# A graph network on one core: the count matrix kept in f16 in DRAM, its row sums made in the convolution

## The chip, the cores and the metric

The kernel runs on one core of one Trainium2 chip. The metric is device time in microseconds. The core has five engines that run in parallel, each in its own order: TensorE (PE, with its weight loads as PEld), VectorE (DVE), ScalarE (ACT), GpSimd (POOL) and SyncE (SP), which here only issues DMAs. GpSimd issues the indirect DMAs. They meet through semaphores.

## What is computed

Four graph layers on 3125 nodes with 256 features and 53125 edges (`src`, `dst`, sorted by `dst`), each with a layer norm and a residual. First two attention convolutions, joined and put through an ELU-like function and a product; then five message-passing layers with batch norm; then the layer that the change also touches; then a gated edge network. What matters here is the third:

```python
def _L2_gnn_ref(x, edge_index, W, b):
    row, col = edge_index[0], edge_index[1]
    h = x @ W + b
    agg = segment_sum(h[col], row, num_segments=n)
    deg = segment_sum(ones, row, num_segments=n)
    return agg * where(deg > 0, 1 / max(deg, 1), 0)[:, None]
```

With a matrix C, in which C[s, d] is the number of edges from s to d, `agg` is C h and `deg` is the row sum of C. The message-passing layers use C as well, the other way round. C has 3200 x 3200 entries after padding (NP = 3200, in NT = 25 tiles of P = 128 nodes).

## The kernel before

The program is a chain of stages. Between them stands a barrier; inside them each engine runs its own list.

1. **Zero and histogram.** SyncE loads `dst` and `x`, then writes zeros over `count_dram`, an f32 matrix of KD = NP * NP entries in DRAM, from a tile `zeros` of 128 x ZF f32 elements that GpSimd sets (NZ = KD / (P * ZF) = 40 writes, loop L205). VectorE and TensorE make a histogram of `dst` meanwhile. VectorE's operations on `iota_row` wait for GpSimd's iotas, which come behind the memset of `zeros`.
2. **Plan and tables.** The edges are put in steps of 128 (S = 440 steps, in G4 = 110 groups of 4), with keys src * NP + dst, and score and attention tables are written to DRAM.
3. **First edge stage** (L670 to L900). For each group GpSimd gathers four blocks of scores (`score_g`, L772) and issues two accumulating scatters into `count_dram` (L792), an element of `number` to an address of `place` for each of 128 edges. Before each scatter it waits for `placed`, the landing of the one before. VectorE finds equal keys and so `number_all` and `place_all`; ScalarE copies them to `number` and `place`.
4. **Second edge stage** (L905 to L1140). The same with four gathers of attention rows (`row_g`, L980) and two scatters (L1000) a group; TensorE and VectorE sum the messages.
5. **Finish of the attention** (L1152 to L1273), five rounds of five tiles. In the first half of a round VectorE makes `val` and `neg` of five tiles (L1213 to L1221), with an exponential on ScalarE in each (L1245) and a transpose on TensorE (L1265). In the second half ScalarE copies `valT` (L1249), TensorE multiplies it with `wu` (L1271) and VectorE adds the result to `x_sb` (L1226), tile by tile: the copy of the next tile needs the next transpose, which TensorE has behind the product. In the same stage the count matrix is converted: SyncE loads a half tile of 128 x 1600 f32 counts (`cnt`, L1180), ScalarE turns it to f16 and sums its rows (`half` and `deg_half`, L1240), SyncE stores it to `by_src` (L1186), 50 times. ScalarE has one such conversion behind each of its exponentials and copies.
6. **Message passing** reads `by_src` as 128 x 25 x 400 f16 pieces.
7. **Convolution** (L1676 to L1770). For each tile SyncE loads 128 rows of `by_src` (`rows`, L1690), TensorE turns them in five pieces (L1703) and multiplies them with the node features (L1708), VectorE takes the pieces from PSUM (`take`, L1752), ScalarE takes the low half of the product (`low_sums`, L1737), and VectorE's `finish(t)` adds the halves (L1756) and adds the result, scaled with a column of `inv_deg`, to `x_sb` (L1758). `inv_deg` is made of `degsrc` for all tiles in the stage ahead.
8. The gated edge network, which also reads `degsrc`.

Of the kernel before, what the change touches and what calls it, by code (L numbers as in the profile page):

```python
# [6 lines left out]
F32 = mybir.dt.float32  # L7
# [9 lines left out]
P = 128  # L17
N = 3125
NT = -(-N // P)
NP = NT * P  # L20
# [16 lines left out]
ZF = 2000  # L37
# [13 lines left out]
HALF = NP // 2  # L51
# [53 lines left out]
def program(nc, a, out):  # L105
# [9 lines left out]
    with top:  # L115
# [47 lines left out]
        zeros = sb("zeros", [P, ZF], F32, early)  # L163
# [14 lines left out]
        count_dram = dram("count_dram", [KD + P, 1], F32)  # L178
        by_src = dram("by_src", [NP, NP], F16)
# [518 lines left out]
        with ExitStack() as ctx:  # L698
# [13 lines left out]
            number = [sb(f"number{q}", [P, 2], F32, ctx) for q in range(2)]  # L712
# [194 lines left out]
        with ExitStack() as ctx:  # L907
            with ExitStack() as inner:
                idx = [sb(f"b_idx{q}", [P, 4], I32, inner) for q in range(2)]
                number = [sb(f"b_number{q}", [P, 2], F32, inner) for q in range(2)]  # L910
# [243 lines left out]
            with ExitStack() as inner:  # L1154
# [6 lines left out]
                cnt = [sb(f"cnt{q}", [P, HALF], F32, inner) for q in range(2)]  # L1161
                half = [sb(f"half{q}", [P, HALF], F16, inner) for q in range(2)]
                deg_half = sb("deg_half", [P, 2, NT], F32, inner)
                cnt_in, stored = [[sem(f"c_{x}{q}") for q in range(2)] for x in ("cnt_in", "stored")]
                halves = [sem(f"c_halves{q}") for q in range(2)]
# [5 lines left out]
                with nc.Block() as block:  # L1171
                    @block.sync
                    def _(sp):
# [8 lines left out]
                        def store(t, q):  # L1182

                            sp.wait_ge(halves[q], t + 1)
                            sp.nop().then_inc(waits_passed, 1)
                            sp.dma_start(by_src[bass.ds(t * P, P), q * HALF:(q + 1) * HALF], half[q][:]).then_inc(stored[q], 16)  # L1186

                        for q in range(2):
                            load(0, q)
                        with sp.Fori(0, NT - 1) as t:  # L1190
                            for q in range(2):
                                store(t, q)
                                load(t + 1, q)
                        for q in range(2):
                            store(NT - 1, q)
                        for q in range(2):
                            sp.wait_ge(stored[q], 16 * NT)
# [1118 lines left out]
```

## Time and profile before

| | us |
|---|---|
| median of 3 runs | 6039.13 (6035.55 to 6039.84) |
| span of the profiled execution | 6027.9 |
| zero and histogram | 0 to 95 |
| first edge stage | about 257 to 1439 |
| second edge stage | about 1446 to 2613 |
| finish of the attention | 2613 to 2840 |
| convolution, from its first transpose | 4068 to 4245 |

The span is the time from the first to the last instruction in one profiled execution; the median holds what lies around it as well. The profile gives an engine's busy time, and for idle time what ended it. A wait is put down to the releaser that came last. The granted clock of TensorE is given in shares of 2.4 GHz; 0.50 is 1.2 GHz.

### The profile page before, as it was taken

The numbers are of one execution on the slowest core, as the hardware profiler recorded it, in microseconds if no ns is written. First come the engines' busy times: TensorE is split into PE (matmuls) and PEld (weight loads), VectorE is DVE, ScalarE is ACT, GpSimd is POOL, SyncE is SP. The second block draws the span as 40 slices with busy tenths as digits, with TensorE's granted clock in tenths as the row PEclk, the third lists the DMA queues.
The fourth block names the chain that finished last, engine by engine and source line by source line (L and its number), as shares of the span: only waits on it lengthen the run. The fifth ranks groups of instructions, "written<-read, shape, count | busy, mean of one in ns | idle before, by whom it ended". The sixth has DMA issues, their size and how long they took to land. (4 is left out here: it accounts for less than half of the span.)

```text
span 6027.9 us, 68970 instructions
## 1 busy us (share of the span) xinstructions
PE 4119.1 (68%) x15934; PEld 2516.1 (42%) x15935; DVE 2693.6 (45%) x6817; ACT 1040.2 (17%) x2628; POOL 2891.1 (48%) x2297
## 2 busy tenths in 40 slices
PE   4544344444666766743799999979777777777769
PEld 3333333333444434422455555545443434434335
DVE  7555555556666666644120221144333333333327
ACT  0100000001222222235220220220111111111112
POOL 0177777776676766710100000000177777777750
PEclk9855555555777788866899999989866667676669
DMA  8233222323666666666623333203266666666652
GB/s 306 80 45 45 40 37 31 31 34 69 127 131 126 134 125 127 136 200 234 207 89 102 92 101 103 88 29 120 74 127 123 127 122 128 128 125 125 125 113 86
DMA packets 538455, 662.17 MB, mean 110 GB/s; under 512 B 129111, under 2 KB 433417, under 8 KB 538283
## 3 DMA queue, kind: packets, MB, share of 16 engines
q0 software_dynamic: 203232, 257.35, 25.7%
q1 hardware_dynamic: 335179, 404.30, 21.9%
q8 instruction: 19, 0.31, 0.0%
q14 instruction: 25, 0.20, 0.0%
HBM read 513.82 MB, written 147.60 MB: 110 GB/s over the span
## 5 line engine op out<-in xcount | busy, mean ns | idle before, releaser
L1921 POOL DMA_INDIRECT src_rows<-src_dram,m_idx x440 | 434.6, 988 | 1559.2 <-ACT m_idx L1960 1425.8
L1930 POOL DMA_INDIRECT sums_dram<-merged,m_place x440 | 701.5, 1594 | 231.5 <-issue 221.1
L1032 PE MATMUL b_p_out<-msg,b_hot 128*128 128x512 f32 x880 | 635.6, 816 | 164.8 <-DVE msg L1065 164.2
L1990 PE MATMUL p_pre<-dst_part,m_hotT 128*128 x880 | 440.9, 596 | 332.1 <-DVE m_hotT L2029 329.0
L772 POOL DMA_INDIRECT score_g<-score_dram,idx x440 | 528.1, 1200 | 279.2 <-ACT idx L749 145.8
L1372 PE MATMUL p_lo<-cbuf,parts 128*128 128x400 f16 x1750 | 585.4, 335 | 6.7 <-DVE aggT L1392 6.7
L810 PE MATMUL p_in<-ident,score_g 128*16 128x128 f32 x440 | 112.4, 411 | 698.0 <-DMA score_g<-score_dram,idx 698.0
L1373 PE MATMUL p_hi<-cbuf,parts 128*128 128x400 f16 x1750 | 585.1, 334 | 0.0
L980 POOL DMA_INDIRECT row_g<-att_dram,b_idx x440 | 437.6, 995 | 150.9 <-issue 97.2
L1000 POOL DMA_INDIRECT count_dram<-b_number,b_place x220 | 373.5, 1698 | 202.8 <-DMA count_dram<-b_number,b_place 114.1
L1992 PE MATMUL p_pre<-attr_w,attrT 64*128 64x256 f32 x880 | 439.4, 592 | 0.0
L792 POOL DMA_INDIRECT count_dram<-number,place x220 | 359.6, 1634 | 154.6 <-DMA count_dram<-number,place 78.9
L1990 PEld LDWEIGHTS p_pre<-dst_part,m_hotT 128*128 128x128 f32 x880 | 195.3, 267 | 535.2 <-issue 526.0
L1390 DVE TENSOR_TENSOR aggT<-p_hi,low_sb 128x400 f32 x80 | 45.9, 574 | 763.6 <-ACT low_sb L1382 763.6
L1065 DVE TENSOR_TENSOR msg<-row_g,weight 128x512 f32<-128x512 f32 x440 | 301.7, 687 | 137.3 <-ACT weight L958 137.0
L2044 DVE TENSOR_TENSOR m_place<-m_place_f,own_row 128x4 int32<-128x4 f32 x110 | 18.1, 164 | 758.2 <-POOLq L1941 750.0
L2001 PE MATMUL p_merged<-m_msg,m_same 128*128 128x256 f32 x880 | 324.1, 532 | 36.1 <-ACT m_msg L1967 35.9
L810 PEld LDWEIGHTS p_in<-ident,score_g 128*16 128x16 f32 x440 | 41.4, 114 | 726.4 <-DMA score_g<-score_dram,idx 709.6
L853 DVE TENSOR_TENSOR_SCAN run<-pen,run,p_in 16x512 f32<-16x512 f32 x110 | 139.5, 1268 | 451.6 <-PE p_in L810 451.6
L1033 PEld LDWEIGHTS b_p_den<-weight,b_hot 128*128 128x128 f32 x880 | 209.0, 238 | 296.1 <-issue 296.1
L1073 DVE TENSOR_TENSOR acc<-acc,b_p_out 128x512 f32 x440 | 300.6, 683 | 7.9 <-PE b_p_den L1033 2.8
L1992 PEld LDWEIGHTS p_pre<-attr_w,attrT 64*128 64x128 f32 x880 | 184.1, 260 | 232.6 <-issue 232.6
(354 smaller groups left out, 7269.2 us busy)
## 6 DMA issues: line engine op xcount, KB each, us to landing
cbuf<-by_src SPq DMA_DIRECT2D x40, 2500.0 KB, 9.7
pair<-pair_dram SPq DMA_DIRECT2D x110, 512.0 KB
count_dram<-zeros SPq DMA_DIRECT2D x40, 1000.0 KB, 25.0
cnt<-count_dram SPq DMA_DIRECT2D x50, 800.0 KB, 6.0
key_rep<-key_dram SPq DMA_DIRECT2D x110, 256.0 KB
dl_rep<-pair_dram SPq DMA_DIRECT2D x110, 256.0 KB
by_src<-half SPq DMA_DIRECT2D x50, 400.0 KB, 3.2
g_rows<-by_src SPq DMA_DIRECT2D x25, 800.0 KB, 4.3
```

Source lines behind the costliest of these rows:

```text
L772: nc.gpsimd.indirect_dma_start(score_g[q][:, u, :], None, score_dram, bass.IndirectOffsetOnAxis(ap=idx[q][:, u:u + 1].bitcast(U32), axis=0 ...
L792: nc.gpsimd.indirect_dma_start(count_dram, bass.IndirectOffsetOnAxis(ap=place[q][:, n:n + 1].bitcast(U32), axis=0), number[q][:, n:n + 1], ...
L980: nc.gpsimd.indirect_dma_start(row_g[q][:, u, :], None, att_dram, bass.IndirectOffsetOnAxis(ap=idx[q][:, u:u + 1].bitcast(U32), axis=0)).t ...
L1000: nc.gpsimd.indirect_dma_start(count_dram, bass.IndirectOffsetOnAxis(ap=place[q][:, n:n + 1].bitcast(U32), axis=0), number[q][:, n:n + 1], ...
L1032: nc.tensor.matmul(p_out[u][:], hot[q][:, u, :], msg[q][:, u, :], start=True, stop=True)
L1372: nc.tensor.matmul(p_lo[m][:], parts[:, k, m, 1, :], cbuf[q][:, k, :], start=(k == 0), stop=(k == NT - 1))
L1373: nc.tensor.matmul(p_hi[m][:], parts[:, k, m, 0, :], cbuf[q][:, k, :], start=(k == 0), stop=False)
L1921: nc.gpsimd.indirect_dma_start(src_rows[q][:, u, :], None, src_dram, bass.IndirectOffsetOnAxis(ap=idx[q][:, u:u + 1].bitcast(U32), axis=0) ...
L1930: nc.gpsimd.indirect_dma_start(sums_dram[u], bass.IndirectOffsetOnAxis(ap=place[q][:, u:u + 1].bitcast(U32), axis=0), merged[q][:, u, :], ...
L1990: nc.tensor.matmul(p_pre[q][:, u, :], hotT[q][:, u, :], dst_part[:, bass.ds(tiles[u], 1), :].rearrange("p o d -> p (o d)"), start=True, st ...
L1992: r = nc.tensor.matmul(p_pre[q][:, u, :], attrT[q][:, u, :], attr_w[:], start=False, stop=True)
L2001: r = nc.tensor.matmul(p_merged[q][:, u, :], same[q][:, u, :], msg[q][:, u, :], start=True, stop=True)
```

## The change

`count_dram` becomes f16, and `by_src` is only a view of it. The zeros are f16, with ZF = 4000 in 20 writes; `number` is f16 in both edge stages. The conversion in the finish of the attention is gone: its tiles, its loads and stores on SyncE, its operations on ScalarE and the last addition to `degsrc` on VectorE. In the convolution ScalarE sums the rows of each loaded tile (`count_row`, one tile ahead of `low_sums`) into a column of `degsrc`, with a semaphore `counted`; SyncE waits for it before it loads into the buffer again, and `finish(t)` makes `inv_deg` of its own tile with four operations of 128 x 1.

```diff
-ZF = 2000
+ZF = 4000
...
-        zeros = sb("zeros", [P, ZF], F32, early)
+        zeros = sb("zeros", [P, ZF], F16, early)
...
-        count_dram = dram("count_dram", [KD + P, 1], F32)
-        by_src = dram("by_src", [NP, NP], F16)
+        count_dram = dram("count_dram", [KD + P, 1], F16)
+        by_src = count_dram[0:KD, :].rearrange("(p n) o -> p (n o)", p=NP)
...
-            number = [sb(f"number{q}", [P, 2], F32, ctx) for q in range(2)]
+            number = [sb(f"number{q}", [P, 2], F16, ctx) for q in range(2)]
...
-                        def load(t, q):
-                            rows = count_dram[bass.ds(t * (P * NP), P * NP), :].rearrange("(p f) o -> p (f o)", p=P)
-                            sp.dma_start(cnt[q][:], rows[:, q * HALF:(q + 1) * HALF]).then_inc(cnt_in[q], 16)
...
-                        def round_counts(t, q):
-                            act.wait_ge(cnt_in[q], t * 16 + 16)
-
-                            act.wait_ge(stored[q], t * 16)
-                            nc.scalar.activation(half[q][:], cnt[q][:], ACT.Copy, accum_out=column(deg_half[:, q, :], t)).then_inc(halves[q], 1)
-
                         def round_of(i):
                             for u in range(5):
                                 act.wait_ge(neg_ready, i * 5 + u + 1)
                                 nc.scalar.activation(neg[:, u, :], neg[:, u, :], ACT.Exp).then_inc(exp_ready, 1)
-                                round_counts(i * 5 + u // 2, u % 2)
                             for u in range(5):
                                 act.wait_ge(val_turned, 5 + i * 5 + u + 1)
                                 nc.scalar.copy(valT[:, u], p_val[u % 2][:]).then_inc(valT_ready, 1)
-                                round_counts(i * 5 + (u + 5) // 2, (u + 5) % 2)
...
+                        sp.wait_ge(counted, t + 1)
+                        sp.nop().then_inc(waits_passed, 1)
                         sp.dma_start(rows[q][:], by_src[bass.ds(t * P, P), :]).then_inc(rows_in[q], 16)
...
+                    act.nop().then_inc(counted, 2)
+
+                    def count_row(t, q, i):
+                        act.wait_ge(rows_in[q], i * 16 + 16)
+                        act.wait_ge(counted, t + 2)
+                        nc.scalar.activation(row_copy[:], rows[q][:], ACT.Copy, accum_out=column(degsrc, t)).then_inc(counted, 1)
...
-                    source_tiles(act, low_sums)
+                    def work(t, q, i):
+                        count_row(t + 1, 1 - q, i + q)
+                        low_sums(t, q, i)
+
+                    count_row(0, 0, 0)
+                    source_tiles(act, work)
...
                     def finish(t, q):
+                        dve.wait_ge(counted, t + 3)
+                        o.did(nc.vector.tensor_scalar(has_deg[q][:], column(degsrc, t), 0.5, None, ALU.is_ge))
+                        o.link(nc.vector.tensor_scalar(inv_deg[q][:], column(degsrc, t), 1.0, None, ALU.max))
+                        o.link(nc.vector.reciprocal(inv_deg[q][:], inv_deg[q][:]))
+                        o.link(nc.vector.tensor_tensor(inv_deg[q][:], inv_deg[q][:], has_deg[q][:], ALU.mult))
                         dve.wait_ge(low_out, t + 1)
```

ScalarE in a round of the finish of the attention, before; `neg` is the exponential's tile, `half` a converted half tile and `valT` the copy that TensorE waits for:

```order
L1245 ACTIVATE neg<-neg 128x512
L1240 ACTIVATE half,deg_half<-cnt 128x1600
L1245 ACTIVATE neg<-neg 128x512
L1240 ACTIVATE half,deg_half<-cnt 128x1600
L1249 COPY valT<-p_val 128x512
L1240 ACTIVATE half,deg_half<-cnt 128x1600
```

The same place after the change, with the loop's start:

```order
L1209 ACTIVATE neg<-neg 128x512 x5
L1212 COPY valT<-p_val 128x512 x5
L88 UNCONDITIONAL_BRANCH
L88 ISA
L1209 ACTIVATE neg<-neg 128x512
L1208 REGISTER_ALU
```

The conversions between the exponentials and copies are gone, and the copies follow the last exponential directly; the operations that are left keep their order.

ScalarE in the convolution, before; `g_low` is the low half of the product:

```order
L1680 ISA
L1737 ACTIVATE g_low<-g_p_conv 128x256
L1735 REGISTER_ALU
L1737 ACTIVATE g_low<-g_p_conv 128x256
L1680 REGISTER_ALU
```

The same place after; `g_rows` is the loaded tile:

```order
L1697 ISA
L1697 ACTIVATE row_copy,degsrc<-g_rows 128x3200
L1702 ACTIVATE g_low<-g_p_conv 128x256
L1695 ISA
L1696 REGISTER_ALU
L1697 ISA
L1697 ACTIVATE row_copy,degsrc<-g_rows 128x3200
```

A sum of the next tile's rows now stands ahead of each `low_sums`.

VectorE in the convolution, `finish` of a tile and the next `take`, before:

```order
L1752 COPY g_rowsT<-g_p_block 128x640
L1756 TENSOR_TENSOR g_sum<-g_p_conv,g_low 128x256
L69 REGISTER_ALU
L1758 ISA
L1758 SCALAR_TENSOR_TENSOR x_sb<-g_sum,inv_deg,x_sb 128x256
L1751 ISA
L1752 COPY g_rowsT<-g_p_block 128x640
```

The same place after:

```order
L1721 COPY g_rowsT<-g_p_block 128x640
L1724 REGISTER_ALU
L1725 ISA
L1725 TENSOR_SCALAR has_deg<-degsrc 128x1
L1726 TENSOR_SCALAR inv_deg<-degsrc 128x1
L68 ISA
L1727 RECIPROCAL inv_deg<-inv_deg 128x1
L68 REGISTER_ALU
L1728 TENSOR_TENSOR inv_deg<-inv_deg,has_deg 128x1
L68 REGISTER_ALU
L1730 TENSOR_TENSOR g_sum<-g_p_conv,g_low 128x256
...
L1732 SCALAR_TENSOR_TENSOR x_sb<-g_sum,inv_deg,x_sb 128x256
```

Four operations on a column, each linked to the one before, stand ahead of the addition that waits for `g_low`.

## Rows read from the trace of the kernel before

**Rows 1.** The page's first line.
```profile
span 6027.9 us, 68970 instructions
```

**Rows 2.** Window table; stretch, its us, then busy us (instructions) by engine.
```profile
257.00:1439.00 1182.00, 480.74 (x2200) 438.10 (x2200) 637.93 (x1772) 53.72 (x332) 886.73 (x660) 0.50 0.29 37
1446.00:2613.00 1167.00, 796.93 (x2640) 474.75 (x2640) 772.83 (x2226) 258.38 (x990) 811.08 (x660) 0.79 0.63 127
```

**Rows 3.** Waits, 2613 to 2840: waited for, us, times, longest.
```profile
PE p_uni L1271 <- ACT valT L1249: 107.1, 25, 17.8
ACT half L1240 <- DMA cnt<-count_dram: 76.2, 44, 4.1
```

**Rows 4.** Timeline, 0 to 96: start, us, engine, operation [idle before].
```profile
0.86 1.76 POOL L212 MEMSET zeros<- 128x2000 f32 x1 [0.29 <-POOLq L2309]
...
2.88 89.52 SPq L206 DMA_DIRECT2D count_dram<-zeros  x40
...
5.22 0.38 DVE L229 TENSOR_SCALAR lo_i<-dst_i 125x425 int32<-125x425 int32 x1 [0.97 <-DMA dst_i<-in_dst]
...
91.56 0.18 DVE L247 COPY deg<-hist 128x25 f32<-128x25 f32 x1 [3.31 <-PE hist L257]
...
95.05 0.23 DVE L435 TENSOR_SCALAR tri_ex<-iota_row,pidx 25x25 f32<-25x25 f32 x1 [3.31 <-PEq L198]
```

**Rows 5.** Timeline, 2613 to 2650, first half of a round.
```profile
2622.26 0.69 DVE L1213 TENSOR_TENSOR val<-acc,den 128x512 f32 x1 [4.32 <-DMA brow<-in_bu]
...
2624.16 0.63 ACT L1245 ACTIVATE neg<-neg 128x512 f32<-128x512 f32 x1 [30.91 <-DVE neg L1217]
2624.70 1.52 ACT L1240 ACTIVATE half<-cnt 128x1600 f16<-128x1600 f32 x1
...
2635.25 0.69 DVE L1213 TENSOR_TENSOR val<-acc,den 128x512 f32 x1
...
2643.11 3.68 PE L1271 MATMUL p_uni<-wu,valT 128*128 128x256 f32 x8 [16.34 <-ACT valT L1249]
```

**Rows 6.** Timeline, a round's second half; then the stage's last addition.
```profile
2728.58 3.62 PE L1271 MATMUL p_uni<-wu,valT 128*128 128x256 f32 x8 [16.01 <-ACT valT L1249]
...
2732.03 0.60 PE L1265 MATMUL p_val<-ident,val 128*128 128x128 f32 x4
...
2733.30 1.99 PE L1271 MATMUL p_uni<-wu,valT 128*128 128x256 f32 x8 [0.68 <-ACT valT L1249]
...
2735.14 0.60 PE L1265 MATMUL p_val<-ident,val 128*128 128x128 f32 x4
...
2735.45 0.42 DVE L1226 TENSOR_TENSOR x_sb<-x_sb,p_uni 128x256 f32 x1 [2.69 <-PE p_uni L1271]
...
2748.84 0.69 DVE L1213 TENSOR_TENSOR val<-acc,den 128x512 f32 x1 [0.27 <-issue]
...
2830.53 0.42 DVE L1226 TENSOR_TENSOR x_sb<-x_sb,p_uni 128x256 f32 x1 [4.89 <-PE p_uni L1271]
```

**Rows 7.** Window table of 2731 to 2744, columns as in rows 2.
```profile
2731.00:2744.00 13.00, 8.92 (x44) 6.94 (x42) 1.68 (x4) 7.63 (x10) 0.00 (x0) 0.97 0.87 305
```

**Rows 8.** Timeline of the first scatter stage, and its last scatter.
```profile
798.74 1.62 POOL L792 DMA_INDIRECT count_dram<-number,place  x1 [0.37 <-issue]
...
803.85 1.63 POOL L792 DMA_INDIRECT count_dram<-number,place  x1 [0.30 <-issue]
...
804.81 0.17 DVE L865 TENSOR_SCALAR prior<-prior 128x4 f32<-128x4 f32 x1 [0.18 <-DVE prior L861]
...
808.60 1.63 POOL L792 DMA_INDIRECT count_dram<-number,place  x1 [0.32 <-issue]
...
1438.40 1.56 POOL L792 DMA_INDIRECT count_dram<-number,place  x1 [2.11 <-DMA count_dram<-number,place]
```

**Rows 9.** Timeline of the convolution, at a tile's end.
```profile
4142.59 0.38 ACT L1737 ACTIVATE g_low<-g_p_conv 128x256 f32<-128x256 f32 x1 [6.41 <-PE g_p_conv L1708]
...
4143.00 0.42 DVE L1756 TENSOR_TENSOR g_sum<-g_p_conv,g_low 128x256 f32<-128x256 f32 x1 [1.00 <-ACT g_low L1737]
```

More of the change, by code:

```diff
@@ L909, in program @@
                 idx = [sb(f"b_idx{q}", [P, 4], I32, inner) for q in range(2)]
-                number = [sb(f"b_number{q}", [P, 2], F32, inner) for q in range(2)]
+                number = [sb(f"b_number{q}", [P, 2], F16, inner) for q in range(2)]
                 place = [sb(f"b_place{q}", [P, 2], I32, inner) for q in range(2)]
@@ L1160, in program @@
                 valT = sb("valT", [P, 5, 4, P], F32, inner)
[L1161 to L1165, printed above, removed]
                 p_val = [ps(f"p_val{v}", [P, 4, P], F32, inner) for v in range(2)]
@@ L1176, in _ @@
                             sp.dma_start(brow[:, w], a[name].partition_broadcast(P)).then_inc(c_in, 16)
-                        def load(t, q):
-                            rows = count_dram[bass.ds(t * (P * NP), P * NP), :].rearrange("(p f) o -> p (f o)", p=P)
-                            sp.dma_start(cnt[q][:], rows[:, q * HALF:(q + 1) * HALF]).then_inc(cnt_in[q], 16)
[L1182 to L1197, printed above, removed]
                     @block.vector
@@ L1227, in _ @@
                         o.leave(R)
-                        for q in range(2):
-                            dve.wait_ge(halves[q], NT)
-                        nc.vector.tensor_tensor(degsrc[:], deg_half[:, 0, :], deg_half[:, 1, :], ALU.add)
                         dve.wait_ge(x_added, NT)
@@ L1594, in program @@
             g_brow = sb("g_brow", [P, D], F32, ctx)
-            inv_deg = sb("inv_deg", [P, NT], F32, ctx)
-            has_deg = sb("has_deg", [P, NT], F32, ctx)
+            row_copy = sb("row_copy", [P, NP], F16, ctx)
+            inv_deg = [sb(f"inv_deg{q}", [P, 1], F32, ctx) for q in range(2)]
+            has_deg = [sb(f"has_deg{q}", [P, 1], F32, ctx) for q in range(2)]
             p_turn = [ps(f"g_p_turn{v}", [P, 2, P], F32, ctx) for v in range(2)]
@@ L1603, in program @@
             (g_in, g_order, turned, taken, products, hw_ready, high_ready, rest_ready, low_ready, blocks, blocks_out, conv_ready, low_out,
-             x_added) = (sem("g_" + x) for x in (
+             x_added, counted) = (sem("g_" + x) for x in (
                  "in", "order", "turned", "taken", "products", "hw_ready", "high_ready", "rest_ready", "low_ready", "blocks", "blocks_out",
-                 "conv_ready", "low_out", "x_added"))
+                 "conv_ready", "low_out", "x_added", "counted"))
             rows_in = [sem(f"g_rows_in{q}") for q in range(2)]
@@ L1648, in _ @@
                 def _(dve):
-                    o = Order(dve, g_order)
-                    o.did(nc.vector.tensor_scalar(has_deg[:], degsrc[:], 0.5, None, ALU.is_ge))
-                    o.link(nc.vector.tensor_scalar(inv_deg[:], degsrc[:], 1.0, None, ALU.max))
-                    o.link(nc.vector.reciprocal(inv_deg[:], inv_deg[:]))
-                    nc.vector.tensor_tensor(inv_deg[:], inv_deg[:], has_deg[:], ALU.mult)
                     def take(t):
@@ L1757, in finish @@
                         own = x_sb[:, bass.ds(t, 1), :].rearrange("p o d -> p (o d)")
-                        nc.vector.scalar_tensor_tensor(own, sum_sb[q][:], column(inv_deg, t), own, ALU.mult, ALU.add).then_inc(x_added, 1)
+                        nc.vector.scalar_tensor_tensor(own, sum_sb[q][:], inv_deg[q][:, 0:1], own, ALU.mult, ALU.add).then_inc(x_added, 1)
                     def work(t, q, i):
```

4 lines of the change are left out of this document (1 added, 3 removed).

## Prediction

> **What bounds the kernel now.** I read the span first [rows 1]: 6027.9 us. The runs have a median of 6039.1, so 11.2 us lie outside the span; every sum below is made on the span and gets these 11.2 us back at the end. The program is a chain of stages with a barrier between them, so I cut the trace by stage and ask of each stage the change touches what ends last in it.
>
> The two edge stages, which hold all the scatters of counts, are bound by GpSimd's issue. In a window table [rows 2] POOL is busy 886.7 of 1182 us in the first and 811.1 of 1167 us in the second, with 660 instructions in each. Most have 0.30 us of issue in front of them [rows 8], so up to 0.3 x 660 = 198 us come on top: 92% and 86% of the stage.
>
> The stage behind them (finish of the attention, 2613 to 2840) is read from its waits [rows 3]. TensorE waited 107.1 us for ScalarE's copy valT, and ScalarE waited 76.2 us for the counts that it converts. The reader is to see a detour: ScalarE executes in order, its conversions of the count matrix stand between exponentials and copies that TensorE and VectorE need, and each conversion waits for an 800 KB load on a queue that also stores the result. This is the part that ends last there.
>
> In the first stage I looked at who reaches the barrier last [rows 4]: VectorE's last copy starts at 91.56 and lasts 0.18, but SyncE issues zero writes from 2.88 to 92.40 and one more after that; everything restarts at 95.05.
>
> **The change part by part.**
>
> *Count conversion removed.* 50 ScalarE conversions, 50 loads and 50 stores leave, with the final wait. I rebuild one round of five tiles without them. In the first half VectorE makes five tiles. Tile 0 starts at 2622.26 and tile 4 at 2635.25 [rows 5], so four tiles take 12.99 us, and this cadence is not disturbed by the conversions. From a tile's first operation to its exponential on ScalarE it is 1.90 us (2624.16), and that lasts 0.63. ScalarE then copies valT(0) at once, and TensorE starts 0.68 us later (the idle time between a finished transpose and the product that needs its copy [rows 6]). Sum: 12.99 + 1.90 + 0.63 + 0.68 = 16.2 us. Now it is 2643.11 - 2622.26 = 20.85.
>
> The second half is TensorE product, transpose, copy, product, five times [rows 6]. First product to the next transpose: 2732.03 - 2728.58 = 3.45 (the granted clock is at its low level, 1.2 GHz). Then from one transpose to the next where no conversion is in the way: 2735.14 - 2732.03 = 3.11, three times 9.33. Last transpose to last product 1.27 (2733.30 - 2732.03), product to VectorE's addition 2.15 (2735.45 - 2733.30), and to the next round's first operation 0.69 (the addition's 0.42 and 0.27 of idle). Sum 16.9. A round takes 16.2 + 16.9 = 33.1 us. Five rounds without the last 0.69 take 164.8 us; now it is 2830.53 - 2622.26 = 208.3. **Saved: 43.5 us.**
>
> I chose the 3.11 us although the clock decides it. The window from 2731 to 2744 shows a mean granted clock of 0.97, that is nearly all at 2.4 GHz, with TensorE busy 8.92 of 13 us [rows 7]. In the new order it would be busy about 2.4 of every 3.1 us over the same kind of stretch, which is more, so I see no reason for a fall before the burst ends. The bound on the other side is a rival below.
>
> *Zeroing halved.* 20 writes of 1000 KB in place of 40. SyncE's loop took 89.52 us because it is held back by the transfers [rows 4]; half is 45 us, long before VectorE's end at 91.74. The barrier then releases about 0.5 us after VectorE, as it did after SyncE: 92.2 in place of 95.05. Against it stands GpSimd's memset, now 4000 f16 elements in place of 2000 f32 ones. It takes 1.76 us if it goes by bytes and up to 3.5 if by elements, and the iotas behind it would be up to 1.8 us later. VectorE has 0.97 us of idle in front of its work on dst [rows 4], so 0 to 0.8 us of it shows; I take 0.4. **Saved: 2.4 us** (bounds 2.0 and 2.8). Nothing later in the zero writes' shadow is gained: the next stages run by VectorE.
>
> *Scatters add f16.* 440 of them, same indices, same number of descriptors. No row shows an f16 scatter. POOL spends 1.62 us on an f32 one of 4 bytes an element [rows 8]; the stage's last scatter took 1.56. I take no difference for the issue: the nearest row is the f32 scatter itself. For the landing: between the end of one scatter (800.36) and the next (803.85) POOL issues two gathers, 3.5 us, and in the next pair 3.1 us (805.48 to 808.60), while the stage's last scatter, with nothing between it and its forerunner, waited 2.11 us in all. So 1.4 and 1.0 us of later landing would be covered. I take zero, bounds in the rivals.
>
> What lands is shown by that 2.11 us. The Trainium skill ("DMA: Bandwidth & Descriptors", Specifications) says that below 512 B a DMA engine does a read-modify-write. By this rule 4-byte and 2-byte elements stand on the same side and the sum is unchanged; read against this change, it says that halving these bytes buys nothing in the scatters and that a narrower element may not be cheaper. The same page (Anatomy of one DMA) puts about 2.0 us of fixed time on one DMA and the rest on bytes; by this the 256 bytes less are worth nothing, and the trace agrees with the 2.0 us at its 2.11.
>
> *Row sums in the convolution.* 25 ScalarE sums of 128x3200 f16 and 100 VectorE operations of 128x1 are added, and two waits on SyncE's loads. ScalarE waits 6.41 us in each tile for the convolution [rows 9]. Nearest row: a conversion of 1600 elements, 1.52 us [rows 5], so 3200 cost 3.1, with the accumulator's read some 3.4. That fits in 6.41 with 3 us left. The sum runs right behind low_sums of the tile before and is done 3.4 us into the tile's 6.8 (6.41 + 0.38), while TensorE transposes the same rows in five pieces spread over the tile, the last at about 4/5 of it, 5.4 us. So the transposes, not the sum, still free the buffer for the next load, and SyncE's new wait is over when it comes to it. On VectorE finish(t) starts with four dependent small operations, before the wait for low_out, where VectorE now idles 1.00 us [rows 9]. A 128x4 operation takes 0.17 and can idle 0.18 before it for its forerunner [rows 8]: 0.7 to 1.4 us for four. So g_sum comes 0 to 0.4 us later, and the next copies are wanted only when TensorE needs their PSUM buffer, later still. Cost 0. If none of it were hidden: 25 x 1.4 = 35 us; if the half of it, 18. Four such operations on 128x25 leave the stage ahead, where VectorE waits for TensorE; nothing.
>
> **Sum.** 6027.9 - 43.5 - 2.4 = 5982.0, with the 11.2 us 5993.2.
>
> **The rivals.**
>
> *Later landing, slower.* If an f16 element's read, add and write took longer than an f32 one's, POOL would wait before every scatter. The decision point: about 1.2 us of margin on average, plus 46/440 = 0.1 us, so a landing 1.3 us later than now eats the whole gain. At 2.0 us later it costs 0.8 x 440 = 352 us, time 6345; at 1.6 us, 176 us and 6169. The last is the price I give it. Against it: a packet of one element hardly depends on its width. Chance 0.07. A dearer issue by 0.1 us on POOL has the same decision point and is counted here.
>
> *Clock stays low in the bursts, no change.* If the shorter bursts ran wholly at 1.2 GHz, each tile of the second half would cost 3.45 + about 1.75 = 5.2 us in place of 3.11; four of these add 8.4 us a round, 42 us in five, and leave 1.5 of the 43.5. Time 6035. Against it: the rise comes within 3.5 us of a burst's start now, and a denser burst should not be later. Chance 0.05.
>
> *Convolution longer.* The small operations or the row sum are on the path after all, by the 18 to 35 us above: 6011 to 6028, and I price it at 25, 6018. The 1.00 us of idle is small, which speaks for it; that TensorE does not wait for g_sum speaks against. Chance 0.06.
>
> *Cheaper scatters.* If the issue fell by 0.1 to 0.6 us each, 44 to 260 us would go: 5949 to 5733. Nothing in the rows asks for it. Chance 0.04.
>
> **How the numbers follow.** My forecast has 0.78. Its own range is 5980 to 6006: up by a clock that falls before the last product of each round (5 x 1.7) and the memset, down by faster round starts and a shorter wait for the bias loads. The given range, 5975 to 6021, takes in the convolution rival and leaves out the scatter ones and the clock. A measurement of this kernel tells 0.2%, some 12 us, from no change. Faster: 0.78 + 0.06 + 0.04 = 0.88; same 0.05; slower 0.07.
>
> **What would show it.** In the profile of the changed kernel: the span from the first val to the last addition near 165 us, ScalarE's wait for DMA gone there and TensorE's wait for valT near 0.7 a tile and longer once a round, at its start; the second stage starting near 92.6; POOL 1.62 us for a scatter, and both edge stages at 1182 and 1167 us within 5; the convolution's tile cadence unchanged, TensorE without gaps. I would be wrong through the scatters first: 440 of them multiply any error, and no row of before shows one in f16.

## The result and the profile after

| | before | after |
|---|---|---|
| median | 6037.34 us, 4 runs (6028.37 to 6039.84) | 6174.56 us, 4 runs (6164.00 to 6185.29) |
| ratio | | 1.0234, 95% interval 1.0217 to 1.0251 |
| span of the profiled execution | 6027.9 | 6166.6 |

The change costs 2.3% where I had forecast a gain of 46 us. The page's first line, to set against [rows 1]:

```profile
span 6166.6 us, 68631 instructions
```

The window table of the two edge stages, columns as in [rows 2]:

```profile
257.00:1526.00 1269.00, 480.74 (x2200) 437.98 (x2200) 638.23 (x1772) 53.57 (x332) 887.46 (x660) 0.50 0.29 35
1532.00:2791.00 1259.00, 806.24 (x2640) 478.62 (x2640) 773.72 (x2226) 258.41 (x990) 809.64 (x660) 0.76 0.64 118
```

Both stages are longer by some 90 us, and GpSimd (POOL) has no more work: 887.46 us for 886.73 and 809.64 for 811.08. The only engine with visibly more is TensorE in the second stage, 806.24 us for 796.93, at a granted clock of 0.76 for 0.79. So the time is waiting. These are GpSimd's waits for the landing of the scatter before (waited for, us, times, longest). Before, second stage, then first; these rows were there to be read and stand in no group ahead of the prediction:

```profile
POOL count_dram L1000 <- DMA count_dram<-b_number,b_place: 114.1, 35, 6.5
POOL count_dram L792 <- DMA count_dram<-number,place: 78.9, 19, 8.1
```

After:

```profile
POOL count_dram L999 <- DMA count_dram<-b_number,b_place: 193.8, 38, 17.5
POOL count_dram L791 <- DMA count_dram<-number,place: 160.1, 19, 14.8
```

The number of waits is nearly the same (19 and 19, 35 and 38); each is longer. These rows do not hold all of the stalls. The profile puts one long wait of each stage down to "issue"; the longest wait in that row went from 6.1 to 11.8 us in the first stage. After:

```profile
POOL count_dram L791 <- issue: 81.0, 201, 11.8
```

The timeline of GpSimd shows one of the stalls. Before:

```profile
811.82 1.73 POOL L772 DMA_INDIRECT score_g<-score_dram,idx  x1 [0.30 <-issue]
819.16 1.63 POOL L792 DMA_INDIRECT count_dram<-number,place  x1 [5.61 <-DMA count_dram<-number,place]
```

The same place after:

```profile
843.67 2.04 POOL L771 DMA_INDIRECT score_g<-score_dram,idx  x1 [0.30 <-issue]
859.94 1.63 POOL L791 DMA_INDIRECT count_dram<-number,place  x1 [14.23 <-DMA count_dram<-number,place]
861.87 0.98 POOL L771 DMA_INDIRECT score_g<-score_dram,idx  x1 [0.30 <-issue]
...
864.42 1.62 POOL L791 DMA_INDIRECT count_dram<-number,place  x1 [0.31 <-issue]
```

The scatter at 859.94 waits 14.23 us for its forerunner, the one at 864.42 nothing but the issue. In both kernels such stalls stand at 12 places of the first stage and 13 of the second, some 9 groups apart, and the scatters between them land in time.

The stages from first to last start, read from the rows of each line (us; "scatters" runs from a stage's first scatter to its last, "landing" is GpSimd's wait above without what is put down to "issue", "finish" runs from the first `val` to the last addition to `x_sb`). e1 to e15 are the experiments below, one profiled execution each:

| | stage 1, scatters | landing | stage 2, scatters | landing | finish | span |
|---|---|---|---|---|---|---|
| before | 1161.4 | 78.9 | 1132.1 | 114.1 | 208.3 | 6027.9 |
| after | 1248.1 | 160.1 | 1222.1 | 193.8 | 168.3 | 6166.6 |
| e1 f16 scatter alone | 1244.7 | 158.7 | 1232.3 | 202.9 | 176.3 | 6189.3 |
| e2 f32 scatter, rest changed | 1155.7 | 73.8 | 1144.4 | 116.0 | 170.8 | 5988.0 |
| e3 two f16 | 1150.9 | 69.2 | 1131.8 | 110.8 | 171.0 | 5955.2 |
| e4 one f16 every 4 bytes | 1158.0 | 76.6 | 1131.0 | 107.4 | 168.2 | 5974.8 |
| e5 matrix in 41 MB | 1248.3 | 157.7 | 1222.5 | 191.9 | 167.8 | 6158.4 |
| e6 rows of 4800 | 1244.4 | 161.0 | 1213.0 | 180.8 | 170.4 | 6150.4 |
| e7 f32, rows of 6400 bytes | 1157.9 | 76.7 | 1134.1 | 119.5 | 170.5 | 5985.9 |
| e8 one scatter a group | 964.0 | 15.8 | 880.7 | 28.7 | 171.0 | 5541.5 |
| e9 odd halves | 1144.2 | 62.0 | 1123.8 | 102.0 | 170.5 | 5947.1 |
| e10 pairs | 1188.1 | 44.0 | 1094.9 | 73.7 | 168.4 | 5945.1 |
| e11 plain write | 1108.3 | 163.5 | 1077.9 | 190.1 | 168.2 | 5875.3 |
| e12 slots 512 bytes apart | 1091.7 | 3.1 | 1037.7 | 18.8 | 170.3 | 5820.1 |
| e13 before, slots 512 | 1093.1 | 3.2 | 1035.0 | 16.9 | 203.9 | 5862.3 |
| e14 slots 4 | 1158.8 | 74.0 | 1133.7 | 112.8 | 168.3 | 5981.6 |
| e15 slots 64 | 1093.1 | 4.3 | 1038.0 | 18.1 | 167.8 | 5816.5 |

From before to after the two stages add 86.7 and 90.0 us, the way from the last scatter's issue to the first `val` 9.3 (19.2 to 28.5; the last scatter turned out to be one of the slow ones), and the finish gives back 40.0. The stretch from the last addition to the convolution adds 5.0, and the one behind the convolution gives 12.2, which no part of the change asks for (it lies between 1756 and 1785 us over the runs here). The first scan starts 0.3 us earlier. Together these make 138.5 of the 138.7 us.

### The profile page after: what moved, and what is told of

Its sections match the earlier page's. It is cut to its first block and busy times, and to the rows that moved or that the text cites. A ratio compares the mean times of both kernels' runs of the same rounds, so it can differ in the third digit from the quotient of the medians.

```text
span 6166.6 us, 68631 instructions
## 1 busy us (share of the span) xinstructions
PE 4129.4 (67%) x15934; PEld 2522.1 (41%) x15935; DVE 2705.2 (44%) x6912; ACT 1034.6 (17%) x2578; POOL 2895.3 (47%) x2297
## 5 line engine op out<-in xcount | busy, mean ns | idle before, releaser
L999 POOL DMA_INDIRECT count_dram<-b_number,b_place x220 | 372.0, 1691 | 294.2 <-DMA count_dram<-b_number,b_place 193.8
L791 POOL DMA_INDIRECT count_dram<-number,place x220 | 358.3, 1629 | 241.1 <-DMA count_dram<-number,place 160.1
L1975 PEld LDWEIGHTS p_merged<-m_msg,m_same 128*128 128x128 f32 x880 | 223.7, 267 | 137.8 <-ACT m_msg L1941 61.6
```

The lines of the kernel that those rows point to most:

```text
L791: nc.gpsimd.indirect_dma_start(count_dram, bass.IndirectOffsetOnAxis(ap=place[q][:, n:n + 1].bitcast(U32), axis=0), number[q][:, n:n + 1], ...
L999: nc.gpsimd.indirect_dma_start(count_dram, bass.IndirectOffsetOnAxis(ap=place[q][:, n:n + 1].bitcast(U32), axis=0), number[q][:, n:n + 1], ...
L1975: r = nc.tensor.matmul(p_merged[q][:, u, :], same[q][:, u, :], msg[q][:, u, :], start=True, stop=True)
```

## The experiments

Where only one time is given, the version was run once. What decides then is the stages: the first stage takes 1144 to 1161 us in the versions that turn out like before, and 1244 to 1248 in those that turn out like after (leaving aside e8, e10 and e11, which change the work in it, and the last experiments, which take the stalls away).

### Which part, and which property of the element

The runs of before that belong to these have a median of 6021.57 us (6011.87 to 6047.95, 7 runs).

**e1**, the scatter alone:

```diff
--- before
-ZF = 2000
+ZF = 4000
...
-        zeros = sb("zeros", [P, ZF], F32, early)
+        zeros = sb("zeros", [P, ZF], F16, early)
...
-        count_dram = dram("count_dram", [KD + P, 1], F32)
+        count_dram = dram("count_dram", [KD + P, 1], F16)
...
-            number = [sb(f"number{q}", [P, 2], F32, ctx) for q in range(2)]
+            number = [sb(f"number{q}", [P, 2], F16, ctx) for q in range(2)]
...
-                cnt = [sb(f"cnt{q}", [P, HALF], F32, inner) for q in range(2)]
+                cnt = [sb(f"cnt{q}", [P, HALF], F16, inner) for q in range(2)]
```

> The kernel before with only the count matrix, its zeros and the numbers that are added in f16; the conversion stage stays (it loads f16 and stores by_src), the row sums stay in it. Theory scatter (the loss is wholly in the edge stages, where the periodic stalls of GpSimd grow): first to last scan about 1244 us (before 1158) and second edge stage about 1220 us (before 1130), span 6028 + 177 - 1 = about 6204, perhaps 10 to 20 less as the loads are halved. Rival (the loss comes from the missing conversion or the row sums in the convolution): span within 10 of 6028.

Measured: one run of 6191.0 us, stages 1244.7 and 1232.3. The whole loss is in the stages with the scatters. The finish of the attention came as a surprise: with all 50 conversions in place it took 176.3 us, against 208.3. Its row of waits, to set against the second of [rows 3]:

```profile
ACT half L1240 <- DMA cnt<-count_dram: 3.2, 5, 0.8
```

So the conversions as such were cheap. What they cost before was ScalarE's wait for the 800 KB loads, 76.2 us in all, and with loads of half the bytes 73 us of that wait are gone.

**e2**, everything but the scatter, with the zeros f32 again in 40 writes:

```diff
--- changed
-ZF = 4000
+ZF = 2000
...
-        count_dram = dram("count_dram", [KD + P, 1], F16)
-        by_src = count_dram[0:KD, :].rearrange("(p n) o -> p (n o)", p=NP)
+        count_dram = dram("count_dram", [KD + P, 1], F32)
+        by_src = count_dram[0:KD // 2, :].rearrange("(p n) o -> p (n o)", p=NP).bitcast(F16)
...
-            number = [sb(f"number{q}", [P, 2], F16, ctx) for q in range(2)]
+            number = [sb(f"number{q}", [P, 2], F32, ctx) for q in range(2)]
```

> The changed kernel with f32 counts: matrix, zeros (2000 elements, 40 writes) and numbers are f32; no conversion, row sums in the convolution. by_src is the first half of the f32 matrix read as f16, so it holds other values. Theory scatter: edge stages as before (1158 and 1130 us), the finish of the attention about 40 us shorter, convolution 161.6 us: span 6028 - 40 = 5988, time about 5996 (my prediction without its 2.4 us for the zeros: 5995.6). Rival (the rest of the change costs it): above 6100.

Measured: 5979.76 us (5968.05 to 5989.74, 4 runs), ratio 0.992 (0.9889 to 0.9951); the profiled span is 5988.0, as expected. Without the f16 scatters the forecast holds.

**e3** and **e4**, the element:

```diff
--- changed, e3
-        count_dram = dram("count_dram", [KD + P, 1], F16)
+        count_dram = dram("count_dram", [KD + P, 2], F16)
...
-            number = [sb(f"number{q}", [P, 2], F16, ctx) for q in range(2)]
+            number = [sb(f"number{q}", [P, 2, 2], F16, ctx) for q in range(2)]
...
--- changed, e4
+        count_dram = dram("count_dram", [2 * (KD + P), 1], F16)
...
-                        nc.scalar.copy(place[q][:], place_all[:, bass.ds(j * 4, 2)])
+                        nc.scalar.mul(place[q][:], place_all[:, bass.ds(j * 4, 2)], 2.0)
```

> The changed kernel with a scattered element of two f16 (4 bytes, the count twice) in a matrix of twice the columns, 41 MB as before's, 40 zero writes; by_src is its first half, so it holds other values. Theory width (an accumulating element of 2 bytes makes the stalls long, one of 4 bytes does not): edge stages as before, 1158 and 1130, time about 5998. Theory type (the f16 addition): stages 1244 and 1220, time about 6175. Theory layout (the denser matrix of 20 MB): as theory width here, since the addresses are those of before.

> The changed kernel with a scattered element of one f16 (2 bytes) at every fourth byte of a matrix of 41 MB (ScalarE doubles the places as it copies them), 40 zero writes; by_src is its first half, so it holds other values. Theory width: stages 1244 and 1220, time about 6175. Theory type: the same. Theory layout: stages as before, 1158 and 1130, time about 5998.

Measured: 5956.85 and 5976.50 us, both with stages as before's. The times lie 41 and 21 us under the numbers given for them; 22 and 9 us of that are behind the convolution, where nothing was changed. e4 adds 2-byte f16 elements and is not slow: neither the type nor the width does it. What e4 shares with before is where the elements lie.

### Where the elements lie

The runs of before that belong to these: 6021.82 us (6009.59 to 6031.89, 7 runs).

```diff
--- changed, e5
-        count_dram = dram("count_dram", [KD + P, 1], F16)
+        count_dram = dram("count_dram", [2 * KD + P, 1], F16)[0:KD + P, :]
--- changed, e6
-KD = NP * NP
+KS = 4800
+KD = NP * KS
...
-                    o.link(nc.vector.scalar_tensor_tensor(key_row[:], src_f[:], float(NP), seg_row[:], ALU.mult, ALU.add))
+                    o.link(nc.vector.scalar_tensor_tensor(key_row[:], src_f[:], float(KS), seg_row[:], ALU.mult, ALU.add))
--- e2, e7
-KD = NP * NP
+KS = 1600
+KD = 21 * P * 2000
...
```

> The changed kernel, whose f16 matrix is the first half of a DRAM tensor of 41 MB, so that other tensors lie as far off as before; nothing else. Theory density (the stalls grow because the scattered elements lie in 20 MB, rows of 6400 bytes): edge stages 1244 and 1222 as in the changed kernel, time about 6175. Theory allocation (where the tensors lie to each other): 1155 and 1131, about 5975.

> The changed kernel with padded rows: a row of the f16 matrix has 4800 elements (9600 bytes), of which 3200 are used; keys are src * 4800 + dst, 30 zero writes of 1000 KB, 31 MB in all. Theory density: less than in the changed kernel, stages between 1155 and 1244 and between 1131 and 1222; if the stall goes with the density, near the middle, time about 6075. Theory row stride (6400 bytes is the bad value): stages as before, time about 5975. Theory allocation: says nothing firm, since the size changes too.

> The kernel of the f32 run without conversion (the rest of the change alone, profiled span 5988), with keys src * 1600 + dst: f32 elements, rows of 6400 bytes, 21.5 MB, 21 zero writes; counts of different edges fall on the same element, so it holds other values. Theory density or row stride: edge stages 1244 and 1222, time about 6165. Theory width after all (2-byte elements packed next to each other are what is slow): 1152 and 1140 as in the f32 run, time about 5985.

> The changed kernel with one scatter a group in place of two (the second is left out, so half of the counts are missing): 5 indirect DMAs a group. It tells what the stall's period counts; in the changed kernel it is one per 9.1 groups, 55 DMAs of 128 descriptors or 18 scatters. Theory descriptors: one stall per 11 groups, 10 in a stage. Theory scatters: one per 18 groups, 6 in a stage. Theory time: one per about 100 us.

Measured: e5 6160.18 us, e6 6155.35 (6150.73 to 6173.17, ratio 1.0231, 1.0208 to 1.0255), e7 5987.56. The theory of allocation fell with e5. Density fell twice: e6 spreads the matrix over 31 MB and stays as slow as after, e7 packs f32 into 21.5 MB and stays as fast as before. The row stride fell with them: e6 has rows of 9600 bytes and is slow, e7 has rows of 6400 and is not.

e8 (one scatter a group, 5543.15 us) agreed with none of its theories as a whole. Nearly all long stalls of the first stage were gone. One wait for a landing of over 3 us is left there (four in the second, of 3.2 to 10.9 us):

```profile
961.96 1.62 POOL L793 DMA_INDIRECT count_dram<-number,place  x1 [12.19 <-DMA count_dram<-number,place]
```

That one scatter should stall for 12.19 us and its neighbours not at all pointed to something in its data.

### Alignment, and the addition

The runs of before that belong to these: 6011.04 us (6000.39 to 6020.98, 9 runs). I still took 2-byte elements next to each other in the matrix for the cause, and asked whether it is their alignment.

```diff
--- e4, e9
-KD = NP * NP
+KS = 2500
+KD = 16 * P * ZF
...
-                        nc.scalar.mul(place[q][:], place_all[:, bass.ds(j * 4, 2)], 2.0)
+                        nc.scalar.activation(place[q][:], place_all[:, bass.ds(j * 4, 2)], ACT.Copy, bias=1.0, scale=2.0)
--- changed, e10 (core)
-                        o.link(TT(same[:], key_rep[q][:], here.unsqueeze(2).broadcast_to(spread), ALU.is_equal))
+                        o.link(TT(offs[:], key_rep[q][:], key_step[:, grp].unsqueeze(2).broadcast_to(spread), ALU.subtract))
+                        o.link(nc.vector.scalar_tensor_tensor(same[:], offs[:], 1.0, offs[:], ALU.subtract, ALU.mult))
+                        o.link(TS(same[:], same[:], 1.0, None, ALU.is_lt))
--- changed, e11
-                                number[q][:, n:n + 1], None, compute_op=ALU.add).then_inc(placed, 16)
+                                number[q][:, n:n + 1], None).then_inc(placed, 16)
```

> The changed kernel with a scattered element of one f16 in every 4 bytes, always the upper half (place 2 * key + 1), rows of 2500 such slots, 33 MB; the places are what differs from the run with one f16 apart, and by_src is not what was scattered, so it holds other values. Theory alignment (an accumulated element whose address is 2 beyond a multiple of 4 is what is slow; in the changed kernel about half are): all are slow, edge stages at least 1244 and 1222 and up to 1330 and 1310, time 6165 to 6350. Rival packing (two different elements in one 4-byte word are what is slow): 1155 and 1131, time about 5970.

> A version that might beat both: the f16 matrix stays dense (20 MB) but is scattered in aligned pairs of 4 bytes (place = key / 2, element = counts of the even and the odd column); VectorE finds edges of the same pair with three more large operations in the first edge stage, ahead of the scan, where it waits for TensorE 4.9 us a group. Theory alignment: edge stages 1155 and 1131, time about 5965. Rival: VectorE's added 2.4 us a group are not hidden: first stage up to 1420, time up to 6230; or the stalls stay whatever the alignment: 6175.

> The changed kernel whose scatters write f16 counts and don't add (counts of an edge in two steps are overwritten). Theory that the narrow access itself is slow, read or write: edge stages 1244 and 1222, time about 6160. Theory that only the adding of a misaligned element is: 1155 and 1131, time about 5965, perhaps less if adding costs something at all.

Measured: e9 5948.78 us, as fast as any so far, so alignment fell. e10 5955.53 us (5946.77 to 5960.56), ratio 0.9908 (0.9895 to 0.9922): 0.9% faster than before, though its first stage grew by 27 us over before's while GpSimd waited 35 us less there for landings; VectorE's extra work was not wholly hidden. e11 5877.00 us, and its timeline says two things at once:

```profile
779.47 0.94 POOL L771 DMA_INDIRECT score_g<-score_dram,idx  x1 [0.30 <-issue]
795.26 0.99 POOL L791 DMA_INDIRECT count_dram<-number,place  x1 [14.85 <-DMA count_dram<-number,place]
```

A scatter that only writes takes GpSimd 0.99 us in place of 1.63, which is the whole gain (440 x 0.64 = 282 us, against 284 in the two stages). The stalls are about as long as with the addition (landing 163.5 and 190.1 us for 160.1 and 193.8), so the adding is not what makes them.

### Where the stalls stand

With type, width, place, alignment and addition gone I looked at the data. The plan cuts the edges, sorted by `dst`, in chunks of 128. A chunk that straddles two tiles of 128 nodes is processed once for each, and the edges of the other tile are masked: their counts go to a slot of their own behind the matrix (L493 to L499 of the changed kernel; `v1` is 0 for a masked edge, `own` is the edge's number in its chunk, 0 to 127):

```python
o.link(nc.vector.scalar_tensor_tensor(key_row[:], src_f[:], float(NP), seg_row[:], ALU.mult, ALU.add))
...
o.link(TT(key_row[:], key_row[:], own, ALU.subtract))
o.link(nc.vector.scalar_tensor_tensor(key_row[:], key_row[:], -float(KD), v1[:], ALU.add, ALU.mult))
o.link(TT(key_row[:], key_row[:], own, ALU.add))
o.did(TS(key_row[:], key_row[:], float(KD), None, ALU.add))
```

That is element KD + own, so the slots lie one beside the other. An edge that repeats an earlier one of its step goes to the same slots (`own_place`), but there are only 143 of those, at most 4 in a step. The 24 boundaries of tiles and the end give 49 of the 440 steps masked edges, 3195 in all (counted from `dst`), and a boundary comes every 440/25 = 17.6 steps, of which each stage scatters two in four: one busy place per 8.8 groups in each stage. Counting the scatters in both timelines, every wait of over 2.4 us ahead of a scatter (a stage's first one aside) follows the scatter of a step with 20 or more masked edges. Some of the first stage:

| step of the scatter before | masked edges | wait before | wait after |
|---|---|---|---|
| 88 | 37 | 2.90 | 3.99 |
| 124 | 50 | 2.51 | 4.74 |
| 53 | 76 | 5.59 | 8.05 |
| 89 | 91 | 5.80 | 10.65 |
| 269 | 103 | 4.95 | 12.50 |
| 197 | 120 | 5.61 | 14.23 |
| 17 | 123 | 4.35 | 14.85 |

After, the wait grows by (14.85 - 3.99) / (123 - 37) = 0.13 us with each masked edge; a straight line through the 34 scatters of both stages with 30 or more masked edges has 0.14 (correlation 0.98). Before, there is no such rate: the wait is 2.9 us at 37 masked edges, 5.6 at 76 and anything from 4.0 to 8.1 at 103 to 123, and the same line has 0.02 (correlation 0.50).

The row of e8 fits: it follows the scatter of group 76, whose first step has 115 masked edges, the only first step with so many. The four waits left in e8's second stage follow steps with 52, 62, 104 and 71. And the spacing sorts all runs so far: slots 2 bytes apart (after, e1, e5, e6, e11) are slow; slots 4 bytes apart (before, e2, e3, e4, e7, e9) are less so. e10 has it milder still (landing 44.0 and 73.7): its pairs put the masked edges of even number 4 bytes apart and send those of odd number to `own_place`, 8 bytes apart.

### Only the slots

The runs of before that belong to these: 6031.03 us (6018.51 to 6042.54, 9 runs). One number, the spacing SP of the slots in elements, is all that differs from the changed kernel (256, 2 and 32 in e12, e14, e15) or from before (128 in e13):

```diff
-        count_dram = dram("count_dram", [KD + P, 1], F16)
+        count_dram = dram("count_dram", [KD + P * SP, 1], F16)
...
-                    o.link(TT(key_row[:], key_row[:], own, ALU.subtract))
+                    o.link(nc.vector.scalar_tensor_tensor(key_row[:], own, -float(SP), key_row[:], ALU.mult, ALU.add))
...
-                    o.link(TT(key_row[:], key_row[:], own, ALU.add))
+                    o.link(nc.vector.scalar_tensor_tensor(key_row[:], own, float(SP), key_row[:], ALU.mult, ALU.add))
...
-                    o.link(TS(own_place[:], pidx[:], float(KD), None, ALU.add))
+                    o.link(TS(own_place[:], pidx[:], float(SP), float(KD), ALU.mult, ALU.add))
```

> The changed kernel (dense f16 counts) with the slots of masked and repeated edges 512 bytes apart in place of 2. Theory slots: the stalls of 13 to 15 us vanish, GpSimd's long waits for count_dram with them; edge stages about 1090 and 1065 (1158 and 1132 less 12 stalls of 5 to 6 us each), time about 5840. Rival (the stalls have another cause): 1244 and 1222, time about 6160.

> The kernel before (f32 counts, conversion) with the slots 512 bytes apart in place of 4. Theory slots: its stalls of 4 to 6 us vanish too, edge stages about 1090 and 1065, time about 6011 - 68 - 67 = 5876. Rival: no change, 6011.

> The changed kernel with the slots 4 bytes apart; the matrix stays dense f16. Theory slots: edge stages as before's (1155 and 1130), time about 5965. Rival (the matrix's own packed elements are slow): 1244 and 1222, time about 6160.

> The changed kernel with the slots 64 bytes apart. Theory slots, if writes that fall on the same 64 bytes are what is slow: as with 512 bytes, time about 5840. If the whole region of 8 KB is still narrow: between 5840 and 5965. Rival: 6160.

Measured:

| | us | ratio to before |
|---|---|---|
| e12, changed, 512 bytes | 5811.60 (5807.90 to 5827.16, 5 runs) | 0.9644 (0.9626 to 0.9662) |
| e13, before, 512 bytes | 5863.25 (5858.26 to 5865.64, 4 runs) | 0.9724 (0.9706 to 0.9742) |
| e14, changed, 4 bytes | 5983.27 | |
| e15, changed, 64 bytes | 5818.17 | |

GpSimd's waits in e12, second stage, then first:

```profile
POOL count_dram L1000 <- DMA count_dram<-b_number,b_place: 18.8, 17, 2.3
POOL count_dram L792 <- DMA count_dram<-number,place: 3.1, 2, 2.4
```

And its timeline where after has the stall of 14.23 us; the scatter at 779.28 is the one behind step 197:

```profile
774.10 1.62 POOL L792 DMA_INDIRECT count_dram<-number,place  x1 [0.30 <-issue]
776.03 0.98 POOL L772 DMA_INDIRECT score_g<-score_dram,idx  x1 [0.30 <-issue]
777.32 1.66 POOL L772 DMA_INDIRECT score_g<-score_dram,idx  x1 [0.30 <-DMA count_dram<-number,place]
779.28 1.63 POOL L792 DMA_INDIRECT count_dram<-number,place  x1 [0.30 <-issue]
```

The stages came out as the slot theory has it in all four runs, and no run came near the rival's numbers. The times miss the numbers given to the fast side in e12 (28 us), e13 (13) and e15 (22), and e14's one run lies 18 us above, with its stages at 1158.8 and 1133.7. From after to e12 GpSimd waits 160.1 - 3.1 = 157 us less for landings in the first stage, which got 1248.1 - 1091.7 = 156 shorter. From before to e13 it waits 76 and 97 us less in the two stages, which got 68 and 97 shorter. e12 beats both kernels, before by 3.6% and after by 5.9% (5811.60 / 6174.56, medians of different times).

The trace's records of single DMA packets tell where in a slow scatter the time lies. Of the scatter behind step 197 in after, all 128 two-byte packets start between 2.2 and 3.5 us from GpSimd's issue, and the last has ended by 3.5. The 16 marks by which the landing is told then come one after another from 6.2 to 18.7 us. In e12 the packets of the same scatter start between 2.2 and 2.8 us, and the seven marks that were recorded stand between 2.7 and 3.1. So most of the stall lies behind the last packet, ahead of the landing marks.

## Why the prediction was wrong, point by point

- **Scatters add f16, the landing at zero: the step that failed.** I took the landing from one scatter, the stage's last, at 2.11 us, and gave every scatter a cover of 1.0 to 1.4 us. That holds for nearly all of them: the back-to-back waits at the stages' ends are still 2.1 to 2.3 us, and GpSimd's 1.62 us is 1.63. But 49 steps hold masked edges, and behind the fuller ones GpSimd waits up to 8.1 us in before and up to 17.5 after. Over both stages the landing rows grew by 160.1 - 78.9 = 81 and 193.8 - 114.1 = 80 us, where the sum had zero. The row of 78.9 us in 19 waits, with a longest of 8.1, is the one I didn't read: an average wait of 4 us says that the 2.11 us scatter is not typical of those that make GpSimd wait. "No row shows an f16 scatter" was true, but the margin of 1.0 to 1.4 us came from the nearest rows, and those show ordinary scatters only.
- **The rival "later landing, slower"** gave 6169, near the 6174.56, by another mechanism. It priced 440 landings, each 1.6 us later. The runs show 12 places in the first stage and 13 in the second with some 7 us more each, and nothing at the others. That the size came out right is luck, and its argument against, that a packet of one element hardly depends on its width, is right by e4.
- **The rule of the Trainium skill on small elements** ("DMA: Bandwidth & Descriptors", Specifications: a read-modify-write below 512 B). I had read it so that 4 and 2 bytes stand on one side and cost alike. The element alone does cost alike (e4). Which targets are written together is what cost here, and the spacing was no term of the prediction. The same page's figure of about 2.0 us of fixed time for one DMA (Anatomy of one DMA) is near the 2.1 to 2.3 us that GpSimd waits behind the issuing instruction of an ordinary scatter. Counted from that instruction's start it is 3.7 us (2.11 + 1.57), and the masked steps are far above either.
- **Count conversion removed: right.** Predicted first `val` to last addition 164.8 us, measured 168.3, a gain of 40.0 for 43.5. The rows of the first round after:

```profile
2808.08 0.69 DVE L1186 TENSOR_TENSOR val<-acc,den 128x512 f32 x1 [2.69 <-DMA brow<-in_bu]
...
2824.14 3.72 PE L1233 MATMUL p_uni<-wu,valT 128*128 128x256 f32 x8 [11.55 <-ACT valT L1212]
2827.69 0.60 PE L1227 MATMUL p_val<-ident,val 128*128 128x128 f32 x4
...
2830.80 0.60 PE L1227 MATMUL p_val<-ident,val 128*128 128x128 f32 x4
...
2841.14 0.69 DVE L1186 TENSOR_TENSOR val<-acc,den 128x512 f32 x1 [0.30 <-issue]
...
2929.52 3.78 PE L1233 MATMUL p_uni<-wu,valT 128*128 128x256 f32 x8 [0.67 <-ACT valT L1212]
...
2976.42 0.42 DVE L1199 TENSOR_TENSOR x_sb<-x_sb,p_uni 128x256 f32 x1 [2.68 <-PE p_uni L1233]
```

  A round is 2841.14 - 2808.08 = 33.06 us (predicted 33.1), its first half 16.06 (16.2), and from transpose to transpose 3.11, as predicted. The 3.5 us missing are mostly in products that run at the low clock. They take 3.78 us in place of 1.99, at each later round's first and, in the fourth round, at the second too (2929.52; the granted clock is 0.50 from 2924 to 2928 and 1.00 from 2934 to 2942). So the rival *clock stays low in the bursts* was wrong but for that one product. TensorE's wait for `valT` is 71.5 us, and the five starts of a round make up most of it.
- **What the detour consisted of** I had only half. e1 shows that 32 of the 40 us come with loads of half the size and the conversions left in; the conversions themselves are worth 8.
- **Zeroing halved: right.** The rows:

```profile
0.86 3.43 POOL L211 MEMSET zeros<- 128x4000 f16 x1 [0.29 <-POOLq L2283]
...
4.55 35.20 SPq L205 DMA_DIRECT2D count_dram<-zeros  x20
...
93.61 0.23 DVE L434 TENSOR_SCALAR tri_ex<-iota_row,pidx 25x25 f32<-25x25 f32 x1 [0.31 <-PEq L197]
```

  The memset takes 3.43 us for as many bytes as took 1.76 before, so it met its upper bound. The next stage starts at 93.61 (predicted 92.6). The first scan starts at 267.2 after 267.5, which looks as if nothing came of it. But that start moves by several us between executions: it lies at 263.3 to 268.2 in the nine profiles with 20 zero writes (mean 265.8) and at 266.8 to 268.5 in the five with 40 (mean 267.8). On average some 2 us are gained, near the 2.4 of the sum.
- **Convolution: right.** First to last `low_sums` takes 161.6 us in both. Rows of a tile after, to set against [rows 9]:

```profile
4286.47 0.16 DVE L1728 TENSOR_TENSOR inv_deg<-inv_deg,has_deg 128x1 f32<-128x1 f32 x1
...
4286.70 0.38 ACT L1702 ACTIVATE g_low<-g_p_conv 128x256 f32<-128x256 f32 x1 [3.34 <-PE g_p_conv L1666]
4286.98 2.86 ACT L1697 ACTIVATE row_copy<-g_rows 128x3200 f16<-128x3200 f16 x1
...
4287.19 0.42 DVE L1730 TENSOR_TENSOR g_sum<-g_p_conv,g_low 128x256 f32<-128x256 f32 x1 [0.56 <-ACT g_low L1702]
4289.74 0.19 ACT L1697 ACTIVATION_READ_ACCUMULATOR row_copy<-g_rows  x1
```

  The sum takes 2.86 and 0.19 us (predicted 3.4 together) and leaves ScalarE 3.34 us of waiting; the four small operations are done by 4286.63, and VectorE still waits 0.56 us for `g_low`.
- **Cheaper scatters** did not come with f16. It came with the addition left out (e11), which is no longer the same computation.
- **The 11.2 us outside the span** were no constant of the kernel. They are the difference between the median of before's runs and the span of one profiled execution. After's profiled run has 6168.27 us for its span of 6166.6, so 1.7 us lie outside.

With the slots apart, the change is worth about what was forecast, by the medians: 5863.25 - 5811.60 = 52 us, against 46.

## What to carry to other kernels

Read the longest wait and the count of a row beside its sum. If a DMA is mostly in time and late by many microseconds at regular places, find out what the data of those places have in common before any price is put on the DMA. Dummy targets of a scatter (masked lanes, repeats, trash rows) should not be packed side by side. In this kernel that cost 2.8% with 4-byte elements and about twice that with 2-byte ones, and slots 64 bytes apart (2-byte elements) or 512 (either) took the stalls away. When an element is narrowed, everything that is addressed in elements draws together, its dummy slots too.

## What the runs showed of the hardware

- Scattered writes to neighbouring addresses within one indirect DMA land late. At 2 bytes apart GpSimd's wait grows by some 0.13 us for each of up to 126 elements. At 4 bytes it is 2.5 to 8.1 us behind a step with 30 or more masked edges (before), with no clear rate. At 64 or 512 bytes no wait is over 2.4 us. The packet records put most of the time behind the last packet, ahead of the landing marks. Whether engines or memory hold it, no run here tells, nor at which spacing between 4 and 64 bytes it ends.
- The stalls are about as long when the DMA only writes and doesn't add (e11). To GpSimd it matters, 1.63 us for issuing an adding scatter and 0.99 for a writing one.
- GpSimd's memset of 4000 f16 elements takes 3.43 us, that of 2000 f32 ones, the same bytes, 1.76.
- From profile to profile the same work behind the convolution takes 1756 to 1785 us. The times of single runs here can't tell less than those 30 us; the edge stages can.
